# Expert-row gathers on GpSimd: eight at once, the others behind steps of the shared expert

## What is computed

```python
logits = jnp.einsum('btc,ec->bte', x, router_w)
top_vals, top_idx = jax.lax.top_k(logits, TOP_K)          # TOP_K = 2 of 16 experts
gates = jax.nn.sigmoid(top_vals)
...
gate, up = jnp.split(jnp.einsum('nc,ech->neh', xf, gate_up_w), 2, axis=-1)
out_all = jnp.einsum('neh,ehc->nec', jax.nn.silu(gate) * up, down_w)
moe = jnp.einsum('ne,nec->nc', w_full, out_all)
shared = (silu(x @ shared_gate_w.T) * (x @ shared_up_w.T)) @ shared_down_w.T
x = x + moe + shared
```

## Time and profile before

| | |
|---|---|
| Median of 3 runs | 1411.06 us |
| Lowest, highest | 1407.27, 1411.35 us |
| Span of the profiled execution | 1379.5 us |
| Busy, of the span | PE 91%, DVE 64%, ACT 48%, Pool 38% |
| Experts phase | from 1157 us of the span to its end |

### The profile page before, as it was taken

One profiled execution on the slowest core, in us unless ns is written; L12 is line 12 of the kernel. 1 busy time (PEld: TensorE's weight loads), 2 busy tenths in 40 slices (PEclk: granted clock), 3 DMA queues, 4 the chain that ended last, 5 costly groups with the idle time before them and its releaser, 6 DMA issues. The chain is left out here.

```text
span 1379.5 us, 18247 instructions
## 1 busy us (share of the span) xinstructions
PE 1255.7 (91%) x5694; PEld 569.1 (41%) x5694; DVE 888.8 (64%) x2045; ACT 663.2 (48%) x1243; POOL 523.9 (38%) x731
## 2 busy tenths in 40 slices
PE   6898989989999999999999999998899888999996
PEld 3232433323343224453453444443242334666663
DVE  5889789788877986458557567568768423233332
ACT  2355455566555655556546556446656551012221
POOL 4444251163312411326217227225423122456665
PEclk9799999999999999999999999999999999999998
DMA  8472513324330333033123123124622004934341
GB/s 262 131 245 81 159 49 96 109 65 147 110 106 24 108 93 108 22 87 108 47 63 108 47 62 108 47 62 123 139 85 48 17 16 118 337 99 55 55 54 16
DMA packets 113216, 131.53 MB, mean 95 GB/s; under 512 B 17017, under 2 KB 93305, under 8 KB 112867
## 3 DMA queue, kind: packets, MB, share of 16 engines
q1 hardware_dynamic: 102867, 119.91, 30.0%
q0 software_dynamic: 10256, 10.45, 4.6%
HBM read 83.25 MB, written 48.40 MB: 95 GB/s over the span
## 5 line engine op out<-in xcount | busy, mean ns | idle before, releaser
L1288 DVE TENSOR_REDUCE Mx<-bank 128x1 f32<-128x512 f32 x512 | 339.0, 685 | 206.6 <-PE bank L1022 204.5
L904 ACT ACTIVATE prob<-bank 128x512 f32<-128x512 f32 x576 | 332.4, 594 | 257.2 <-PE bank L1048 255.6
L1048 PE MATMUL bank<-QS,KS 99*128 99x512 bf16 x768 | 296.1, 387 | 40.1 <-ACT prob L904 19.5
L1022 PE MATMUL bank<-KS,QS 96*128 96x512 bf16 x768 | 296.9, 388 | 14.2 <-DVE Mx L1285 8.0
L1061 PE MATMUL bank<-prob,V 128*17 128x512 f32 x1536 | 206.6, 610 | 0.7 <-ACT prob L904 0.7
L904 ACT ACTIVATE prob<-prob 128x512 f32<-128x512 f32 x192 | 120.9, 629 | 159.4 <-DVE prob L1299 158.5
L1048 PEld LDWEIGHTS bank<-QS,KS 99*128 99x128 bf16 x768 | 74.8, 98 | 234.2 <-ACT prob L904 130.3
L1022 PEld LDWEIGHTS bank<-KS,QS 96*128 96x128 bf16 x768 | 76.0, 99 | 123.0 <-issue 47.2
L1285 DVE CUSTOM_DVE_ANT_0 bank<-bank,ff_h 128x512 f32<-128x512 f32 x128 | 87.9, 696 | 20.6 <-PE bank L1022 20.0
L741 POOL TENSOR_SCALAR parts<-rest 128x512 bf16<-128x512 f32 x47 | 29.1, 620 | 183.4 <-DVE rest L1248 182.8
L727 POOL TENSOR_SCALAR shift<-mv 128x4 f32<-128x4 f32 x28 | 5.5, 197 | 233.5 <-DVE mv L1209 233.5
(11 more groups left out here) (180 smaller groups left out, 1833.2 us busy)
## 6 DMA issues: line engine op xcount, KB each, us to landing
stack_scr<-parts SPq DMA_DIRECT2D x48, 384.0 KB, 2.6
QS<-stack_scr SPq DMA_DIRECT2D x47, 384.0 KB, 4.1
KS<-stack_scr SPq DMA_DIRECT2D x47, 384.0 KB, 5.0
stack_scr<-parts SPq DMA_DIRECT2D x48, 256.0 KB, 2.9
w_gu<-in_gate_up SPq DMA_DIRECT2D x16, 512.0 KB, 9.6
stack_scr<-parts SPq DMA_DIRECT2D x48, 128.0 KB, 2.9
cT<-in_ctxT SPq DMA_DIRECT2D x8, 512.0 KB, 5.8
w_dn<-in_down SPq DMA_DIRECT2D x16, 256.0 KB, 10.0
```

The source lines that it names most:

```text
L904: act.activation(prob[:, u % NP_, j, :], src, ACT.Exp, scale=CAST).then_inc(exp_done, 1)
L1022: pe.matmul(m, QS[0:STACK, h, qt * P:(qt + 1) * P], KS[0:STACK, h, :], start=True, stop=True).then_inc(s_full, 1)
L1048: pe.matmul(bankT[e % NT][:, :], KS[0:ROWS, h, kt * P:(kt + 1) * P], QS[0:ROWS, h, :], start=not on_pe, stop=True).then_inc(t_full, 1)
L1288: dve.tensor_reduce(dst, b, AX.X, ALU.max).then_inc(s_read, 1)
```

## The change

It adds waits ahead of some of the 30 early gathers. LATE is 3, QT and HT are 4, so n_last is 8. The dictionaries come out as: gathers 8, 9, 10, 11 wait for y_read 5, 6, 7, 8 (the four adds of chunk 1); gathers 13, 15, 17 for sg_done 10, 11, 12 (the last three Silus of chunk 2); gathers 20, 21, 22, 23 for y_read 9, 10, 11, 12 (the four adds of chunk 2). Gathers 0 to 7 have no new wait, nor have 12, 14, 16, 18, 19 and 24 to 29, which stand in the queue behind those that have.

```diff
@@ -1517,6 +1517,11 @@
         landings_ready = sem("landings_ready")
         apart = sem("apart")
 
+        n_last = (LATE - 1) * QT
+        after_sum = {8 + i: n_last - QT + 1 + i for i in range(QT)}
+        after_gate = {13 + 2 * i: LATE * HT - HT + 2 + i for i in range(HT - 1)}
+        after_sum.update({20 + i: n_last + 1 + i for i in range(QT)})
+
         tokens_of = t_scr.rearrange("b s n -> (b s) n")
         table_of = tag_scr.rearrange("(r q) c -> r (q c)", q=P)
 
@@ -1575,6 +1580,10 @@
                                             bass.IndirectOffsetOnAxis(token[:, s:s + 1], 0)).then_inc(xr_in[s % ROWS_SEM], 16)
 
                 for s in range(NX):
+                    if s in after_sum:
+                        pool.wait_ge(y_read, after_sum[s])
+                    if s in after_gate:
+                        pool.wait_ge(sg_done, after_gate[s])
                     rows(s)
                 pool.wait_ge(rows_out, 16 * B)
                 for s in range(TILES):
```

## The result

The kernel after takes 1392.19 us in the median of 4 runs (1389.83 to 1394.78), the kernel before 1410.2 (1407.27 to 1411.35): a ratio of 0.987 with a 95% interval of 0.9849 to 0.9891, 18 us faster. The forecast was 1412.0, no change.

What follows compares the result with a forecast made beforehand. The prediction took the start of scatter-add 0 plus Pool's own chain as the bound. A scatter-add 0 later by 0.93 us made the span 1380.4; with 31.56 us carried unchanged the forecast was 1412.0, range 1406.5 to 1416.5.

Steps and rivals of the forecast that it cites:

- 31.56 us over the span, and I carry these unchanged: Whole kernel: the median's 31.56 us beyond the profiled span was added unchanged to the forecast span of 1380.4, giving 1412.0.
- the start of scatter-add 0 plus Pool's own chain: Expert phase: what sets the end; a start d us later moves the end by d.
- The replay of the gathers: Early gathers on Pool: last shared-expert add to scatter-add 0 grows from 8.10 to 9.03 us.
- the early gathers cost the shared expert nothing: Shared expert: PE busy 12.00 of 12 us, so no wait shows that spacing the gathers could remove.
- the forecast's 0.93: Scatter-add 0: starts at 1232.28 instead of 1231.35, the part of the 7.3 us gather delay left uncovered.
- every later product has over 2 us in hand: Expert phase: after tile 0, finished products wait over 2 us for their scatter-adds, so Pool's chain decides.
- Rival C: Shared expert: spaced gathers free DMA share, PE gets operands sooner; 1411.0 at best; chance 0.13 with unseen gains.
- PE's pause of 0.97 us: PE between first gather and tile 0: its one pause, for hid, taken as all PE could regain.
- Rival B: Last six gathers beside the expert loop's DVE copies: Pool is held up, 1415.0 to 1418.1 us; chance 0.08.
- The range of 1406.5 to 1416.5: Whole kernel: low end from 1407.27 and part of the faster rival, high end from 1411.35 + 4.4 and a little.

Runs made afterwards that it cites:

- before_again: The kernel before, unchanged, run once more for a trace from an execution whose own time is known; 1410.14 us, span 1408.7.
- last_half: The kernel after with only the waits before gathers 20 to 23, gathers 0 to 19 at full pitch; ratio to before 0.9918, 1398.17 us.
- behind_weights: The kernel before, but Pool waits until all expert weights have landed before its first gather, then 30 gathers at full pitch; 1407.9 us.
- sixteen_rows: The kernel before, but each early gather fetches 16 of its 128 rows, with a memset of xr ahead of the gathers; 1411.55 us.
- short_filler: The kernel before with one memset of 16 elements between gathers; ratio 0.9991, 1410.75 us.
- four_in_flight: The kernel before with four gather semaphores instead of eight, so at most four gathers are in flight; ratio 0.9901, 1399.28 us.
- eight_filler: The kernel before with eight gathers at full pitch, then a memset of 400 elements ahead of each of the other 22; ratio 0.9857, 1389.57 us.
- ten_first: The kernel after with ten gathers at once instead of eight and the other waits two gathers later; ratio to before 0.9866, 1393.04 us.
- first_half: The kernel after with only the waits before gathers 8 to 11 and 13, 15, 17; ratio to before 0.9886, 1394.99 us.
- after_again: The kernel after, unchanged, run again on the same chip as before_again; ratio to before 0.9868, 1390.58 us, span 1385.9.
- two_in_flight: The kernel before with two gather semaphores, so a gather waits for the landing of the one two before it; 1399.6 us.
- one_filler: The kernel before with one memset of 400 elements between gathers; ratio 0.9856, 1391.38 us.
- paced: The kernel before with three small memsets behind each of the 30 early gathers; 1421.97 us.
- plain_from_pool: The kernel before, but the 30 early gathers are plain transfers of 128 consecutive rows issued by Pool in the same places; 1387.75 us.
- plain_from_sp: The kernel before, but 30 plain transfers of 128 consecutive rows are issued by SP behind the expert weights, with own semaphores; 1387.35 us.

## Why the prediction was wrong

**The step that failed** is "31.56 us over the span, and I carry these unchanged". In every run of the study with both on record, time and span differ by 1.7 to 1.9 us. The account ahead of the prediction, that such a difference is what lies around the span, is wrong for this trace. The 31.6 was no surrounding of the execution. It was the sign that the timed executions contained some 30 us which the trace did not show: 23 in the shared expert, as before_again shows, and about 6 ahead of the phase (1163.5 against 1157.3; the other traces of the study have 1160.6 to 1170.6 there). None of the executions of before, 1404.5 to 1416.06, is near the 1381 that the span of 1379.5 would give. (Why the shown execution was otherwise, I can't tell; one thing that differs in its trace stands in the next section.)

**Point by point.** The bound, "the start of scatter-add 0 plus Pool's own chain", held: 139.9 to 141.1 us from scatter-add 0 to the last start in the traces with whole gathers, whatever stood ahead, but for last_half (142.9). The replay of the gathers held (forecast 9.03, measured 9.05 and 9.02). That the early gathers cost the shared expert nothing, which the prediction took from PE's busy 12.00 of 12 us, failed: the full pitch held back PE's increments, and spreading the gathers took 23.0 us out of the shared expert, of which 1.7 are given back at scatter-add 0. The 1.7 are the forecast's 0.93 and 0.75 by which the last add itself comes late. That leaves some 21 us against 18.0 and 19.6 by the medians; the stage ahead of the phase, which the change doesn't touch, varies by more than this difference from one execution to the next. That "every later product has over 2 us in hand" failed at tile 1, whose product came 0.9 us ahead of its scatter-add instead of 2.56. Rival C had the right sign and the wrong path (DMA share: behind_weights keeps the loss with the weights landed, sixteen_rows with an eighth of the gathers' bytes), and I capped it at PE's pause of 0.97 us, again because the trace showed only that one. Rival B, Pool hindered by DVE, did not occur: the seven gathers beside the expert loop kept 0.94 to 0.95 us. The lock that the Trainium skill tells of (SBUF — State Buffer, "SBUF: two separate sides"), which the page ties to copies within SBUF, does not show beside copies that read PSUM.

The range of 1406.5 to 1416.5 was built from the terms of one trace and could not hold 1392. A rival "the timed executions hold something that this trace lacks, worth up to 30 us" had its number in front of me.

## What stays open

How a train of indirect gathers from Pool holds back PE's increments, and PE itself, isn't shown. The runs narrow it. The table has, for each trace, the pitch of the early transfers, by how much the worst of the 12 adds stands further behind the end of its PE product than the usual 0.04 us, and how many of the 480 landing increments of the 30 early transfers (16 each) are in the trace's record of semaphore updates:

| trace | pitch, us | worst add late by, us | landings recorded, of 480 |
|---|---|---|---|
| before (the one shown first) | 1.25 | 0 | 480 |
| before_again | 1.25 | 24.6 | 70 |
| behind_weights | 1.25 | 24.1 | 97 |
| short_filler | 1.26 | 26.1 | 45 |
| sixteen_rows | 1.14 | 28.8 | 45 |
| four_in_flight | 1.53, then 1.26 | 11.2 | 168 |
| last_half | 20 at 1.25 | 12.7 | 109 |
| eight_filler | 8 at 1.25, then 1.53 | 6.0 | 172 |
| ten_first | 10 at 1.25, then waits | 3.5 | 122 |
| first_half | 8 at 1.25, waits, 13 at 1.25 | 1.5 | 222 |
| after, after_again | 8 at 1.25, then waits | 0.75 | 213, 211 |
| two_in_flight | 1.9, in pairs | 0 | 354 |
| one_filler | 1.53 | 0 | 436 |
| paced | 2.50 | 0 | 436 |
| plain_from_pool, plain_from_sp | 0.72, 0.64 | 0 | 480, 480 |

It takes the indirect form and a pitch of 1.26 us or less; at 1.53 throughout nothing is late. The first increment over 1 us late is due when 7 to 14 gathers of an unbroken train have started, and the last arrives 2.5 to 8 us behind the train's end. PE's increments are late, while DVE's in the same spell are in time. Ruled out as the cause are the gathers' bytes and rows, the weights and other instructions between them; four in flight make it smaller and don't cure it.

The last column is the open rival. Over whole traces the record of semaphore updates is incomplete too (14302 to 14556 updates in those with late increments, 14747 to 14919 in those without, 15414 in the first trace of before), and in the stretch of the train records are lost in nearly the order in which increments are late. The first trace of before has the same train, keeps all of them and has no late increment. So what carries the records may be what holds PE, and then part or all of the gain would be there only in executions that are recorded. Against a plain count of records: plain_from_pool brings the same 480 increments in 21.6 us instead of 37 and loses none; and paced and one_filler lose 44, two_in_flight 126, without a late add. Whether an execution without the recording loses the 20 us isn't tried. The Trainium skill (NOTIFIC — the notification-queue block, "Interfaces") says that the block which writes such records can press back on its producers when an inner buffer fills, and that this can stall an engine; no run here shows that it did.

No version with the full computation beat the kernel after by a measurable amount; one_filler and eight_filler equal it without a wait on another engine.

## What to carry to other kernels

Compare the time of a run with the span of the profiled execution before anything is summed: here they should differ by 2 us, and 31 meant that the trace was of another kind of execution. Where a wait is released by something the profile can't name, look at the producer's products: if they were done long before, the semaphore is late and not the work. And a long train of indirect gathers at Pool's own pace isn't free because its bytes are hidden. In this kernel it paid to stretch it to 1.53 us or to break it behind eight; try both where the slack allows, with the reservation above on recorded executions.

## What the runs showed of the hardware that I had not expected

- PE's semaphore increments arrived up to 24.6 us behind their products beside a train of 30 indirect gathers at 1.25 us (before_again), and in time at 1.53 us (one_filler).
- In such a spell PE started one instruction every 1.40 us for 17 us, with nothing that it waited for in the profile (sixteen_rows).
- 30 plain transfers of the same size from the same queue at 0.72 us had no such effect.
- After PE's pause of 20.65 us its granted clock was 0.50, and eight products of 512 columns took 6.06 us instead of 3.60.
